# Counting edges: three one-hot buffers per group of a window, and one packed register word for two windows

## What is computed

```
deg  = segment_sum(1, dst) + 1;  norm = rsqrt(deg)[src] * rsqrt(deg)[dst]
gcn(h, W, b) = segment_sum(norm * (h @ W)[src], dst) + b, loops added
x = layernorm(x + gcn(relu(gcn(relu(gcn(x, W1, b1)), W2, b2)), W3, b3))
w_m, w_a = edge_attr @ W_msg + b_msg, edge_attr @ W_attn + b_attn   (16x16 per edge)
attn = softmax over the edges of a target of w_a * x[src]
x = layernorm(x + segment_sum(w_m * x[src] * attn, dst).sum(1))
```

## Time and profile before

| | us |
|---|---|
| median of 3 runs (lowest, highest) | 2688.94 (2686.95, 2690.07) |
| the profiled execution | 2685.97 |
| its span, first to last instruction | 2684.2 |
| busy in the span: TensorE, VectorE | 2030.2, 2113.0 |
| busy in the span: ScalarE, GpSimd | 1413.4, 1288.1 |
| mean granted TensorE clock | 0.832 |

### The profile page before, as it was taken

The page is one execution under the profiler, slowest core; times in us unless marked ns, Lnnn a source line. Parts: engine busy times, 40 slices in busy tenths (PEclk is TensorE's granted clock), DMA queues, the critical chain, the costliest instruction groups (busy, mean ns, idle before and its releaser), DMA issues.

```text
span 2684.2 us, 39375 instructions
## 1 busy us (share of the span) xinstructions
PE 2030.2 (76%) x5872; PEld 714.5 (27%) x5873; DVE 2113.0 (79%) x4340; ACT 1413.4 (53%) x4967; POOL 1288.1 (48%) x1556
## 2 busy tenths in 40 slices
PE   3766777777699648887888888888888788888782
PEld 1111111111333313333333333333333333333330
DVE  5876888887401149999999999999999889999883
ACT  5123333321001047777767777777776666766762
POOL 2100000012455477666666666666666665666653
PEclk9655555555898859999999999999999999999996
DMA  2000000000000011110000000101000000100110
GB/s 32 14 0 26 0 0 0 0 0 1 20 11 11 16 13 11 10 10 10 10 9 10 10 10 9 10 10 10 9 10 10 10 9 10 9 10 10 10 7 9
DMA packets 87256, 26.29 MB, mean 10 GB/s; under 512 B 63117, under 2 KB 84223, under 8 KB 87103
## 3 DMA queue, kind: packets, MB, share of 16 engines
q0 software_dynamic: 37824, 18.62, 6.4%
q1 hardware_dynamic: 49327, 6.96, 1.7%
q10 hardware_dynamic: 80, 0.43, 0.1%
HBM read 23.30 MB, written 2.51 MB: 10 GB/s over the span
## 4 chain that ended last, share of the span: by engine, by line
issue 28%; DVE 26%; PE 17%; DVEq 15%; POOL 5%; POOLq 4%; ACT 3%; DMA 1%; ACTq 0%; PEldq 0%; SPq 0%; PEld 0%
PE pair L801 10%; DVE eo L1392 7%; DVEq L1409 3%; DVE top L1407 3%; ACT eo L988 3%; PE bank L658 3%; DVE hot L1132 3%; DVE hot L1130 3%; PE pair L658 2%; DVE top L1410 2%; DVE eo L1430 2%; DVEq L1417 2%; DVE rden L1445 2%; DVEq L1153 2%; PE pw L788 1%
## 5 line engine op out<-in xcount | busy, mean ns | idle before, releaser
L617 POOL DMA_INDIRECT nbr<-table,rec x960 | 963.7, 1004 | 463.1 <-issue 258.2
L801 PE MATMUL pair<-eo,ident 128*128 128x512 f32 x1856 | 903.0, 632 | 123.0 <-DVE eo L1430 120.1
L988 ACT ACTIVATE eo<-pw,nbr 128x32 f32<-128x32 f32 x3776 | 686.9, 407 | 0.0
L801 PEld LDWEIGHTS pair<-eo,ident 128*128 128x128 f32 x1856 | 364.8, 202 | 603.1 <-issue 586.9
L1392 DVE TENSOR_TENSOR eo<-pw,nbr 128x1024 f32 (+1 forms) x357 | 417.0, 1218 | 43.4 <-PE pw L788 42.9
L1130 DVE TENSOR_SCALAR hot<-iota_key,near_key 128x500 bf16<-128x500 f16 x974 | 341.0, 350 | 119.3 <-issue 55.5
L788 PE MATMUL pw<-wk,termsT 100*128 100x512 bf16 x954 | 288.5, 384 | 128.6 <-issue 64.6
L977 ACT ACTIVATE eo<-eo 128x2048 f32<-128x2048 f32 x117 | 223.5, 1910 | 206.1 <-DVE eo L1421 206.1
L658 PE MATMUL bank<-hot 128*128 128x500 bf16 x488 | 230.3, 603 | 127.2 <-DVE hot L1132 103.5
L1430 DVE TENSOR_TENSOR eo<-eo x232 | 273.5, 1221 | 30.9 <-issue 27.1
L658 PE MATMUL pair<-hot 128*128 128x500 bf16 x486 | 228.5, 602 | 51.6 <-DVE hot L1132 45.4
(11 more groups left out here) (237 smaller groups left out, 1834.7 us busy)
## 6 DMA issues: line engine op xcount, KB each, us to landing
nbr<-table,rec POOLq DMA_INDIRECT x960, 2.4
rec<-unit_recs SPq DMA_DIRECT2D x122, 8.0 KB, 1.7
attr<-in_edge_attr_dram,rec POOLq DMA_INDIRECT x120, 2.5
unit_recs<-place SPq DMA_DIRECT2D x27, 64.0 KB, 1.6
shared<-key_row SPq DMA_DIRECT2D x1, 1600.0 KB, 6.7
counts<-in_dst_dram SPq DMA_DIRECT2D x1, 448.0 KB
counts<-in_src_dram SPq DMA_DIRECT2D x1, 448.0 KB
place<-in_src_dram,at_i POOLq DMA_INDIRECT x26, 2.6
```

The source lines that it names most:

```text
L617: pool.indirect_dma_start(nbr[:, b, j * FEAT:(j + 1) * FEAT], None, table, bass.IndirectOffsetOnAxis(ap=rec[:, b, j:j + 1], axis=0)).then_ ...
L801: mm = pe.matmul(total, ident[:], eo[:, ring, j * 2 * CH:(j + 1) * 2 * CH], start=False, stop=(j == SLOT - 1), skip_group_check=True)
L988: done = act.activation(eo[:, ring, lo:lo + wide], pw[:, j - 4, c * wide:(c + 1) * wide], ACT.Copy, scale=nbr[:, held, j * FEAT + c:j * FE ...
```

## The change

- `hot` gets seven slots in place of five: one for each step of a window (`a * GROUP + k`) and one for tail steps. `s_hot_free` starts at 3 (BASE // GROUP), so VectorE may be three groups ahead.
- Start and number of blocks of a window are packed in 14 bits (WORD), those of two windows in one 32-bit word, `win_word`. Each engine loads one word per turn of the loop: TensorE behind the first group of the even window, VectorE behind the first group of the odd window, for the next turn. Start and number are then taken out of the register by shifts and masks.
- `plane_tables` builds the words: a multiply-add, a subtraction, two copies, a shift and an OR. Its scratch row lies in `hot`.
- `edge_key` and `edge_low` shrink from 896 to 822 columns, with their copies on ScalarE. `identh` and its copy go; `add_loops` reads the bf16 identity.

The diff, cut to its core:

```
-        hot = sb("hot", [P, (2 * GROUP + 1) * (NG * WIN + P)], BF16, conv)
-        hot_key = hot[:, 0:(2 * GROUP + 1) * NG * WIN].rearrange("p (k n) -> p k n", n=NG * WIN)
+        hot = sb("hot", [P, (BASE + 1) * NG * WIN + (BASE + 1) * P], BF16, conv)
+        hot_key = hot[:, 0:(BASE + 1) * NG * WIN].rearrange("p (k n) -> p k n", n=NG * WIN)
...
 tensor:
-                                mm = count(at % 2 * GROUP + k, a == 0 and k == 0)
+                                mm = count(a * GROUP + k, hot_low[:, a * GROUP + k, :], a == 0 and k == 0)
                             mm.then_inc(s_hot_free, 1)
-                        n = pe.value_load(win_count[0:1, bass.ds(i * 2 + v, 1)], min_val=1, max_val=DEPTH)
+                            if v == 0 and a == 0:
+                                pe.reg_mov(pe_word, pe.value_load(win_word[0:1, bass.ds(i, 1)], min_val=0,
+                                                                  max_val=(1 << 2 * WORD) - 1))
+                        pe.reg_alu(pe_n, pe_word, v * WORD, ALU.logical_shift_right)
+                        pe.reg_alu(pe_n, pe_n, DEPTH - 1, ALU.bitwise_and)
+                        n = pe.snap(pe.snap(pe_n, min_val=0, max_val=DEPTH - 1) + 1, min_val=1, max_val=DEPTH)
...
 vector:
-            dve.sem_inc(s_hot_free, 2)
+            dve.sem_inc(s_hot_free, BASE // GROUP)
...
-                dve.tensor_copy(win_start[:, 0:NWIN], win_row_g[:, 0, :])
-                dve.tensor_copy(win_count[:], win_row_g[:, 1, :])
+                dve.scalar_tensor_tensor(out=win_row_g[:, 0, :], in0=win_row_g[:, 0, :], scalar=float(DEPTH),
+                                         in1=win_row_g[:, 1, :], op0=ALU.mult, op1=ALU.add)
+                dve.drain()
+                dve.tensor_scalar(win_row_g[:, 0, :], win_row_g[:, 0, :], 1.0, None, ALU.subtract)
+                dve.drain()
+                words = win_row_g[:, 0, :].rearrange("p (i v) -> p v i", v=2)
+                dve.tensor_copy(win_word[:, 0:NWIN // 2], words[:, 0, :])
+                dve.tensor_copy(win_odd[:], words[:, 1, :])
+                dve.drain()
+                dve.tensor_scalar(win_odd[:], win_odd[:], WORD, None, ALU.logical_shift_left)
+                dve.drain()
+                dve.tensor_tensor(win_word[:, 0:NWIN // 2], win_word[:, 0:NWIN // 2], win_odd[:], ALU.bitwise_or)
                 dve.drain().then_inc(s_planes, 1)
...
+            def first_of(v, word):
+                dve.reg_alu(first, word, v * WORD + DEPTH.bit_length() - 1, ALU.logical_shift_right)
+                if v == 0:
+                    dve.reg_alu(first, first, (1 << WORD - DEPTH.bit_length() + 1) - 1, ALU.bitwise_and)
...
                             hot_row.then_inc(s_hot, 1)
+                            if v == 1 and a == 0:
+                                dve.reg_mov(word_next, word_at(i + 1))
                             if a == 1:
+                                first_of(1 - v, word if v == 0 else word_next)
                                 dve.wait_ge(s_hot, w * (2 * BASE // GROUP) + at)
-                                near(i * 2 + v + 1, 1 - v).then_inc(s_near, 1)
-                        n = dve.value_load(win_count[0:1, bass.ds(i * 2 + v, 1)], min_val=1, max_val=DEPTH)
+                                near(i * 2 + v + 1, 1 - v, first).then_inc(s_near, 1)
+                        dve.reg_alu(tiles, word, v * WORD, ALU.logical_shift_right)
+                        dve.reg_alu(tiles, tiles, DEPTH - 1, ALU.bitwise_and)
+                        n = dve.snap(dve.snap(tiles, min_val=0, max_val=DEPTH - 1) + 1, min_val=1, max_val=DEPTH)
...
+                    dve.reg_add(word, word_next, 0)
                     dve.reg_add(windows, windows, 1)
...
-                    dve.tensor_tensor(here, here, identh[:].unsqueeze(1).broadcast_to([P, n, P]), ALU.add)
+                    dve.tensor_tensor(here, here, identb[:].unsqueeze(1).broadcast_to([P, n, P]), ALU.add)
```

More of the change, by code:

```diff
@@ L38 @@
 DEPTH = 16
+WORD = 14
 GROUP = 2
@@ L656, in count_plane, with count @@
                     for v in range(2):
-                        def count(k, first):
-                            return pe.matmul(bank[v][:, 0:NG * WIN], hot_low[:, k, :], hot_key[:, k, :],
+                        def count(k, low, first):
+                            return pe.matmul(bank[v][:, 0:NG * WIN], low, hot_key[:, k, :],
                                              start=first, stop=False, skip_group_check=True)
@@ L841, in _ @@
                 act.wait_ge(s_turned, k + 1)
-                act.copy(to[:], flat[:, 0:EG * P]).then_inc(s_keys, 1)
+                act.copy(to[:], flat[:, 0:NB + DEPTH]).then_inc(s_keys, 1)
             for t in range(FIRST, NT + 1):
@@ L1103, in _ @@
             windows = dve.alloc_register("dve_windows")
+            word, word_next, first, tiles = (dve.alloc_register(f"dve_{v}") for v in ("word", "next", "first", "count"))
             mid = dve.alloc_register("dve_mid")
@@ L1116, in plane_tables @@
                 dve.drain()
-                dve.tensor_copy(win_start[:, 0:NWIN], win_row_g[:, 0, :])
-                dve.tensor_copy(win_count[:], win_row_g[:, 1, :])
-                dve.drain().then_inc(s_planes, 1)
[L1121 to L1126, removed]
@@ new lines, in plane_tables, with near @@
+                dve.drain().then_inc(s_planes, 1)
+            def near(window, v, first):
+                to = dve.snap(first, min_val=0, max_val=NB)
+                key = dve.tensor_scalar(near_key[v][:], edge_key[:, bass.ds(to, DEPTH)], win_off[:, bass.ds(window, 1)],
+                                         None, ALU.add)
+                return dve.tensor_copy(near_low[v][:], edge_low[:, bass.ds(to, DEPTH)])
+            def first_of(v, word):
+                dve.reg_alu(first, word, v * WORD + DEPTH.bit_length() - 1, ALU.logical_shift_right)
+                if v == 0:
+                    dve.reg_alu(first, first, (1 << WORD - DEPTH.bit_length() + 1) - 1, ALU.bitwise_and)
@@ L1132, in one_hot, with word_at, hot_keys, hot_lows @@
+            def word_at(pair):
+                return dve.value_load(win_word[0:1, bass.ds(pair, 1)], min_val=0, max_val=(1 << 2 * WORD) - 1)
+            def hot_keys(slot, v, k):
+                return dve.tensor_scalar(hot_key[:, slot, :].rearrange("p (a d) -> p a d", a=NG), iota_key[:],
+                                         near_key[v][:, k], None, ALU.is_equal)
+            def hot_lows(slot, v, k):
                 return dve.tensor_scalar(hot_low[:, slot, :], iota_low[:], near_low[v][:, k], None, ALU.is_equal)
@@ L1134, in one_hot_plane @@
             def one_hot_plane():
-                near(0, 0)
+                dve.reg_mov(word, word_at(0))
+                first_of(0, word)
+                near(0, 0, first)
                 dve.drain()
```

29 lines of the change are left out of this document (14 added, 15 removed).

## The result

The changed kernel takes 2543.85 us (median of 4 runs, 2543.05 to 2546.82) against 2688.01 us for the kernel before on the same chip (4 runs, 2686.95 to 2690.07): ratio 0.9465, 95% interval 0.9448 to 0.9481. The sign and the place were right, the size was not.

What follows compares the result with a forecast made beforehand. It took a chain over VectorE and TensorE in the counting loop as the bound. 78 x (7.41 - 6.2) = 94, + 5 for tails, - 1 for tables gave 98 us less: 2591 us, range 2562 to 2634.

Steps and rivals of the forecast that it cites:

- Part 1: Counting loop: three buffers per group remove TensorE's lost 0.40 us per window; pair 6.59 us instead of 7.41, low clock.
- Part 2: Counting loop, VectorE's sequencer: packed words leave one register load per pair of four, so VectorE's own pair takes 5.95 us.
- for the rest: VectorE's pair in the counting loop: 0.2 us kept for unnamed remaining holes, beside 0.2 for the loop's branch.
- Part 3: TensorE's clock in the counting loop: rises often and falls again, granted 0.6 to 0.8, mean pair 6.2 us.
- term of the clock: Counting loop: the mean pair of 6.2 us lies above VectorE's own 5.95 because the clock falls back at times.
- rival (b): Counting loop: VectorE bounds everywhere, the clock being high enough; pair 5.95 us, time 2571 us; chance 0.11.
- Part 4: Around the loop: 78 pairs count, tails save 5 us, tables cost 1 us, the whole saving passes on.
- count of pairs: Counting loop: one pair in 79 is hidden by TensorE's wait for ScalarE, so 78 pairs count.
- (a): Counting loop: the clock stays low but for a few windows; pair 6.59 us, time 2621 us; chance 0.29.
- (c): VectorE's sequencer in the loop: register operations put back what the loads took; pair 7.0 us, time 2653 us; chance 0.10.
- (d): VectorE's sequencer becomes the loop's bound through dear register operations; pair 7.96 us, 43 us slower, 2732 us; chance 0.03.

Runs made afterwards that it cites:

- experiments one and two: Kernel before with three buffers per group but old loads: 2877.42 us, ratio 0.9938; then with packed words but two groups of buffers: 2872.76 us, ratio 0.9923.
- clock-alone experiment: Kernel before with one more matmul per window, result thrown away, behind the second group: 2874.58 us, ratio 0.9930.

## Why the prediction was wrong

**What bounds the kernel: right.** A chain over two engines, with the hole inside the window from the second group of buffers and VectorE's own holes from the loads. Both were found in the rows named, and experiments one and two took them away one at a time.

**Part 1: right.** 6.59 us a pair at the low clock; 6.65 was measured at 210 us, where the clock stays low over three windows, and 6.70 at the loop's start. VectorE's own pace without the words, 7.03, came out as 7.02 with the three buffers alone.

**Part 2: the mechanism right, a term too large: the first step that failed.** The added operations cost 44 to 70 ns, as taken from the ALU_OP of the earlier trace rows, and not the 0.19 of the operation behind a load. But I kept 0.4 us per pair, 0.2 for the loop's branch and 0.2 "for the rest", and wrote 5.95 (5.5 + 0.4 is 5.9: the sum was off by 0.05 as well); the lower end that stood beside it, 5.5, is what was measured: 5.49. The sequencer runs ahead of the engine. Its branch and its register operations cost time only where a load had used up the lead, and with the load moved behind the first group they are covered whole. I had seen the holes only in a loop whose lead was gone, and carried a piece of them over to one that has it. Over 78 pairs that is 0.46 x 78 = 36 us.

The load on TensorE in the middle of the even window shows as 0.27 of "issue" there and costs nothing, as said. That losing the loads at its windows' ends could give 0 to 0.05 a pair was too little: they give 14 / 79 = 0.18, and not by a shorter turn.

**Part 3: the second step that failed, in how much and not in kind.** "I expect the clock to rise often, and to fall again, because a TensorE that waits for VectorE is idle more than half the time at the high level", hence 6.2 as a mean between 6.59 and 5.95. Measured was a granted clock of 0.80 to 0.94 in all stretches of 60 us from 180 to 480, with TensorE busy 39 to 40 us of 60. The inference from the earlier trace rows didn't carry over: those 2.23 us of 5 belonged to a TensorE that was handed 9 matmuls in 5 us by a VectorE with holes, 108 in 60; a VectorE without holes hands it 130, a fifth more, and in stretches of 5 us at 1.00 TensorE is busy 2.9 to 3.7. The clock did fall again, as forecast: of the 48 stretches of 5 us from 240 to 480 us, 16 have less than 0.95, the lowest 0.66. But it rose again within a few us each time, and VectorE was busy at least 4.77 of 5 even there. A short low stretch costs VectorE little, because three groups of stock bridge it; where the low level lasted over three windows, near 210 us, VectorE did wait (0.20 and 0.71 us). (That the whole loop before has 0.50 but for a few stretches passes over its first 40 us, where the record has 1.00.) The mean was then not a mean of two paces but nearly VectorE's alone. The term of the clock, 6.2 less 5.95, is 0.25 x 78 = 20 us. With the 36 above this is 56; some 10 of it are given back in the stretches where the pair is slower than 5.49, and that leaves the 46 between 98 and 144. (Taken in the other order the same two terms are 34 for the clock and 22 for VectorE's pace, since the mean mixes them.)

Neither error alone would have missed the range of 2562 to 2634. With 5.49 and the same mixing as in the prediction (0.39 of the way to 6.59) the pair is 5.92 and the time 2569; with the clock right and VectorE at 5.95 it is rival (b), 2571. The range also left out the prediction's own lower end: a pair of 5.5 is 78 x 1.91 + 4 = 153 us, 2536, while 2562 stands for a pair of 5.83.

So rival (b) is what happened, VectorE as the bound nearly everywhere, with the lower end of its pace: 5.49 in place of 5.95. I gave it 0.11, on the ground that the high level had fallen back each time in the kernel before. The clock-alone experiment shows why this was weak evidence: with one matmul more per window the same loop has 0.86 to 0.92 where it had 0.50 to 0.59. The clock hung on how much TensorE was fed. TensorE's two loads put back, with the same matmuls and wider gaps ahead of them, went with a lower clock, so the gaps may count too; the change alters both, and the runs don't part them.

The Trainium skill ("TensorE: Matmul & The Clock Gate", "A second HAM failure mode: psum-queue depth-cycling") was weighed at this place, for small gaps between groups of matmuls that make the clock go up and down at the cost of throughput. Its description fits the packed words with two groups, where one loop ran at 0.50 and at 0.88 by turns and its 10 runs scatter over 42 us (the 23 of the kernel before over 27). In the changed kernel TensorE has gaps of 0.27 to 0.91 us too, and the clock does go up and down, but throughput hardly suffers, because it is set by VectorE: with the clock held at 1.00 the kernel is 4 us faster. The measurement decides: with these gaps the clock didn't stay down for long.

**Part 4: right in what it left out, off in small terms.** Everything behind the loop moved by the same amount to within 3 us (141.7 at the loop's end, 139.6 at the span's). The tables cost 1.0 us: the first near starts at 42.80, and TensorE's first matmul at 44.48 instead of 43.43. The diagonal add in bf16 takes the same 1.90 us as in f16:

```profile
531.28 1.90 DVE L1214 TENSOR_TENSOR counts<-counts,identb 128x3072 f16<-128x3072 f16 x2 [0.33 <-issue]
```

A tail step costs 0.42 now (0.62 before), as worked out. ScalarE didn't become the bound. The count of pairs was off by one: 20 lie ahead of the long wait and 59 behind it (so the 447.82 us of before are 7.59 a pair with tails, not 7.46), and none is hidden, since the wait for ScalarE hardly changes (22.41 and 24.17 us). The sum with measured sizes: 79 x (7.41 - 5.49) = 151.7, + 5.2 for tails, - 1 for the tables, - 1.8 for the wait, - 11.5 for pairs slower than 5.49 (4.8 in TensorE's first 20, 6.7 in the other 59), - 1 since the loop before was a little faster than 7.41 a pair on the mean, gives 141.6 at the loop's end, where 141.7 is read.

**Rivals (a), (c) and (d)** fell. The clock stayed low nowhere for long; the register operations cost 45 ns; the point of 0.185 us per operation from which (d) would decide was not come near.

## What to carry to other kernels

When two engines hold each other up, work out the slower engine's own pace with nothing left over, and see to it that the range reaches it; here it was what came. Two fixes that give 21 and 25 us alone gave 134 together, since each removed the bound that hid the other. Add up an engine's steps from start to start (here 12 x 0.42 + 2 x 0.21) and trust the sum; holes that a sequencer showed where its lead was used up don't come along. And the clock went with what TensorE was fed (0.50 to 0.59, and 0.86 to 0.92 with one matmul more a window): before saying that it will fall again, ask whether the change alters what TensorE was fed where it fell, how long a low stretch would last, and whether the buffers bridge it.

## What the runs showed of the hardware beside this

On two of the chips the kernel before takes 210 us more, and the changed one 221, though the flat part of the loop is the same. Of the 221 the loop's end shows 37 (560.20 against 523.02). These 37 are lost in two places, 57 to 91 us and 496 to 523 us, where GpSimd issues its indirect DMAs, while VectorE stands idle, and TensorE behind it, with "issue" as the cause. The changed kernel from 60 to 85 us, on the first chip and on one of those two:

```profile
60.00:85.00 25.00, 17.20 (x52) 3.99 (x50) 24.78 (x119) 4.80 (x9) 19.21 (x20) 0.93 0.17 48
```

```profile
60.00:85.00 25.00, 6.92 (x17) 0.99 (x15) 7.42 (x32) 1.17 (x3) 18.89 (x20) 0.55 0.18 50
```

VectorE passes 32 instructions in place of 119 in the same 25 us, at nearly the same DMA share; in its timeline a one-hot has 5.86 us of "issue" ahead of it. What holds it up isn't in the trace, and stays open, as does whether the 184 behind the loop have the same cause.

Loads of a register from on-chip memory cost VectorE, as the bound, 0.3 to 0.4 us each (0.83 us for two of near's, 0.60 for two of the number's), though the profile shows the engine idle for only 0.27 and 0.48 of that. And an instruction's shown duration isn't its rate: with the extra matmul in the loop `hot_key` lasts 355 ns on the mean, in the changed kernel 346, with 0.42 us from step to step in both.
